# Two sets of feed-forward buffers, value products in pairs, and another order of loads and stages in a gated cross-attention kernel

## The chip, the cores and the metric

The program runs on one core of a Trainium2 chip. The time is the device time of one launch in microseconds (us), lower is better. Five engines work from queues of their own: TensorE (PE in the profile, its weight loads are PEld), VectorE (DVE), ScalarE (ACT), GpSimd (POOL) and SyncE (SP), which here only starts transfers and waits.

## The reference

Two gated blocks follow each other on x, which has 2 batches of 256 rows of 512 numbers. The context has 2 batches of 512 rows of 512.

```python
x = x + tanh(g_xattn[0]) * matmul(fake_quant(layernorm(x)), fake_quant(ctx))      # first sum
x = x + tanh(g_ffn[0])   * (W_base h + b + 0.5 * inverse_transform(adapters(h)))  # h = layernorm(x)
x = x + tanh(g_xattn[1]) * attention(layernorm(x), ctx, mask)   # 32 heads of 16, 8 key groups
x = x + tanh(g_ffn[1])   * bitlinear(relu(bitlinear(h, w_gate))**2 * bitlinear(h, w_up), w_down)
```

bitlinear rounds its input to 8 bits by the row's largest value, and its weights to -1, 0 and 1 by the mean of their absolute values. The weights are 1376 by 512, three of them.

## The kernel before, in words

The 512 rows are four tiles of 128. A stage is a tuple such as `("y0", 2, 1)`; one list of stages, `schedule()`, is walked by every engine, and each engine issues in that order the instructions that it has in a stage. So the list is the order of work on each engine, and semaphores join the engines. The list has `PREPARATION` first. Then come 128 steps of attention (4 heads of one key group of one tile are 4 steps): `s` makes the scores of one head on TensorE, VectorE reduces them to a maximum, `m` puts the maxima into the operand, `t` makes the scores again, transposed, and ScalarE takes the exponential, GpSimd clears masked places (`keep`) in the later half, and `pv` multiplies by the values. `FILL` says which other stages stand behind which step. Its keys go on above 152, where attention is over: there they only give an order, and I call that part the tail.

The stages that the change touches:

- `vt` multiplies the adapters' coefficients (after masks) by the transform's matrix, `we` multiplies that by the encoders, and VectorE adds the result to `wT`; `y0` uses it.
- `k` and `v` are keys and values; both need `wkvT` and the transposed context `ctx_T`. `ksplit` and `qsplit` split keys and queries into three bf16 parts, which go through DRAM. `qpick` brings the first heads' queries into place without DRAM.
- `cquant` quantises the context, `ln0`, `ln1`, `ln2`, `ln3` are the layer norms, `hT` a transpose.
- `fabs`, `fsum`, `fscale`, `fround`, `fclamp`, `fternary` make the three ternary weights out of `stage_w`, one after the other; `fload` 1 and 2 load the next matrix into the same `stage_w`.
- `f1T`, `gu`, `hidden`, `fq`, `f2T`, `y2`, `y2up` are the last feed-forward part of a tile: transpose the input, gate and up products in three pieces (512, 512 and 352 columns), gate times up and the row's maximum on VectorE, quantise, transpose, down product in three pieces, add to x and store.
- `y1` and `y1up` are the attention's output product and its addition to x.
- `warm` is a run of products of ones that nobody reads.

In the kernel before, a tile's gate values, quantised hidden values and both transposes have one buffer each (`gate`, `hid_q`, `hqT`, `hid_qT`), so a tile's stage waits for the tile before it to have left the buffer. The four down products cannot be put off, since the buffer must be emptied.

```python
if t:
    wait_filled(act, ("y2", t - 1))      # f2T: hid_qT of the tile before has been read
if t and stage[2] == 0:
    act.wait_ge(hid_q_ready, 2 * t)      # gu: gate of the tile before has been quantised
```

## Time and profile before

| what | value |
|---|---|
| median of 3 runs | 285.31 us (283.99 to 285.43) |
| the profiled execution | 285.12 us, span 283.3 us |
| mean granted TensorE clock | 0.976 of full speed |
| PE, DVE, ACT, POOL busy | 262.0, 211.9, 185.3, 115.4 us |
| bytes moved | 27.56 MB |
| first `s` matmul, last `pv` matmuls | 64.57 us, 244.35 us |

A time in a row is counted from the start of the span. The profile's lines name source lines: L622 is `vt`, L681 `q`, L706 `k`, L716 `v`, L671 `y0`, L738 `s`, L760 and L763 `t`, L787 `pv`, L810 `y1`, L828 `gu`, L836 `f2T`, L847 `y2`, L613 `warm` on PE. A float matmul stands as two instructions in the trace, so `vt`, which has four, is shown as x8. "Idle before" is the time for which the engine stood before an instruction, and what ended it.

### The profile page before, as it was taken

To read this page: it belongs to the slowest core of one execution; us is meant where nothing else is said; L and a number is where in the kernel's file an instruction comes from. 1 tells how busy PE (TensorE), PEld (TensorE's weight loads), DVE (VectorE), ACT (ScalarE), POOL (GpSimd) and SP (SyncE) were. 2 spreads that over 40 slices of the span, in tenths; PEclk is the share of its full clock that TensorE was granted. 3 is DMA by queue.
4 is the path that set the end of the run, shared out by engine and by line. 5 is a ranking of instruction groups with operands and counts; after the bars stand their busy time and mean duration, and the time that the engine had idled before them with its cause. 6 is when DMAs were issued, how large, how long until landed. Compare 5 with 4: busy or idle time off the path is not lost.

```text
span 283.3 us, 5004 instructions
## 1 busy us (share of the span) xinstructions
PE 262.0 (92%) x1617; PEld 128.4 (45%) x1640; DVE 211.9 (75%) x612; ACT 185.3 (65%) x311; POOL 115.4 (41%) x171
## 2 busy tenths in 40 slices
PE   8499899788899999999999999999999999899894
PEld 8326358545443343374244275324244253256581
DVE  3777956668887399886969962989988555969682
ACT  3602389568488989786589785888598577452232
POOL 3003304826311055575556475769646556100000
PEclk9879799999799999999999999999999999999999
DMA  6999945150592800057600000800001000000000
GB/s 182 410 409 417 373 191 111 38 102 21 132 364 81 141 0 2 1 194 281 102 0 3 0 2 3 156 9 1 5 0 39 0 0 3 0 37 2 37 2 37
DMA packets 7665, 27.56 MB, mean 97 GB/s; under 512 B 1344, under 2 KB 3952, under 8 KB 5880
## 3 DMA queue, kind: packets, MB, share of 16 engines
q1 hardware_dynamic: 7208, 21.55, 25.8%
q0 software_dynamic: 288, 5.70, 5.2%
q8 instruction: 13, 0.21, 0.3%
q14 instruction: 12, 0.10, 0.1%
q10 hardware_dynamic: 144, 0.00, 0.0%
HBM read 23.79 MB, written 3.41 MB: 96 GB/s over the span
## 4 chain that ended last, share of the span: by engine, by line
PE 73%; DVE 10%; ACT 10%; issue 5%; DMA 1%; POOL 0%; DVEq 0%; ACTq 0%
PE bank L760 10%; PE bank L787 10%; PE bank L738 10%; PE bank L671 5%; PE bank L681 5%; PE bank L828 5%; PE bank L763 4%; PE bank L810 4%; PE bank L847 3%; PE bank L746 3%; PE bank L706 2%; ACT big L968 2%; PE bank L613 2%; PE bank L622 2%; PE bank L716 2%
## 5 line engine op out<-in xcount | busy, mean ns | idle before, releaser
L1194 DVE CUSTOM_DVE_ANT_0 junk<-bank,maskb 128x512 bf16<-128x512 f32 x128 | 83.9, 687 | 19.7 <-PE bank L738 18.9
L968 ACT ACTIVATE big<-bank 128x512 f32<-128x512 f32 x128 | 74.5, 596 | 27.1 <-PE bank L760 11.6
L549 POOL TENSOR_TENSOR big<-big,product 128x512 int32<-128x512 int32 x48 | 61.6, 1284 | 49.6 <-ACT big L968 49.2
L738 PE MATMUL bank<-kst,qst 96*128 96x512 bf16 x128 | 48.9, 386 | 2.4 <-DVE mx L1194 1.6
L760 PE MATMUL bank<-qst,kst 99*128 99x512 bf16 x128 | 49.5, 386 | 0.9 <-ACT qst L951 0.5
L787 PE MATMUL bank<-big,vp 128*32 128x512 f32 x256 | 33.7, 604 | 1.5 <-POOL big L549 0.5
L738 PEld LDWEIGHTS bank<-kst,qst 96*128 96x128 bf16 x128 | 12.6, 99 | 33.9 <-issue 24.9
L763 PE MATMUL bank<-ident_b,maskb 128*128 128x512 bf16 x65 | 24.7, 380 | 0.0
L951 ACT ACTIVATE qst<-bank 3x512 bf16<-3x512 f32 x32 | 18.9, 590 | 7.0 <-PE bank L746 6.4
L760 PEld LDWEIGHTS bank<-qst,kst 99*128 99x128 bf16 x128 | 12.5, 98 | 21.8 <-ACT big L968 6.6
L828 PE MATMUL bank<-ternary,hqT 128*128 128x512 bf16 (+1 forms) x95 | 20.7, 356 | 1.2 <-ACT hqT L985 1.0
L559 POOL TENSOR_TENSOR mx<-mx 128x4 f32<-128x4 f32 x64 | 13.1, 204 | 20.8 <-DVE mx L1194 18.6
L671 PE MATMUL bank<-wT,hT 128*128 128x512 f32 x32 | 17.2, 644 | 2.5 <-ACT hT L908 1.7
L613 PE MATMUL bank<-ones_b 128*128 128x128 bf16 x280 | 18.3, 230 | 1.1 <-POOL ones_f L504 1.1
L613 PEld LDWEIGHTS bank<-ones_b 128*128 128x128 bf16 x280 | 17.7, 104 | 2.4 <-issue 1.1
L593 POOL TENSOR_SCALAR stage_w<-stage_w,wscale 128x1376 f32<-128x1376 f32 (+1 forms) x12 | 17.9, 1496 | 0.0
L681 PE MATMUL bank<-hT,wqT 128*128 128x128 f32 x128 | 17.3, 284 | 0.1
L681 PEld LDWEIGHTS bank<-hT,wqT 128*128 128x128 f32 x128 | 16.6, 198 | 1.1
L938 ACT ACTIVATE ternary<-stage_w 128x1376 bf16<-128x1376 f32 (+1 forms) x12 | 16.2, 1350 | 0.0
L810 PE MATMUL bank<-woT,aT 128*128 128x512 f32 x32 | 15.4, 592 | 0.0
L572 POOL TENSOR_TENSOR x<-x,product 128x512 f32<-128x512 f32 x3 | 3.9, 1307 | 25.4 <-ACT product L893 25.4
L828 PEld LDWEIGHTS bank<-ternary,hqT 128*128 128x128 bf16 x96 | 9.0, 97 | 10.9 <-ACT hqT L985 1.8
(167 smaller groups left out, 403.2 us busy)
## 6 DMA issues: line engine op xcount, KB each, us to landing
stage_w<-in_w_down POOLq DMA_DIRECT2D x1, 2816.0 KB, 11.5
stage_w<-in_w_gate SPq DMA_DIRECT2D x1, 2752.0 KB, 21.7
stage_w<-in_w_up POOLq DMA_DIRECT2D x1, 2752.0 KB, 12.1
...
```

The lines of the kernel that those rows point to most:

```text
L549: nc.gpsimd.tensor_tensor(p, p, keep[:, nt, KEEP_ST.index(i):KEEP_ST.index(i) + 1, :].broadcast_to([P, HG, P]), ALU.mult).then_inc(kept, 1)
L613: i = mm(o[:, 0:P], ones_b[:, :], ones_b[:, :], start=True, stop=True)
L671: i = mm(o[:, :], hT[:, k, :], wT[:, k, :], start=(k == 0), stop=(k == KT - 1))
L681: i = mm(o[:, c * P:(c + 1) * P], wqT[:, k, c * P:(c + 1) * P], hT[:, k, :], start=(k == 0), stop=(k == KT - 1))
L738: mm(o[:, :], qst[0:KS, tile % 2, g * HG + hh, :], kst[0:KS, tb(tile)[0], g, :], start=True, stop=True).then_inc(fill(stage), 1)
L760: i = mm(o[:, :], kst[0:KM, b, g, s * P:(s + 1) * P], qst[0:KM, tile % 2, g * HG:(g + 1) * HG, :], start=True, stop=by_keep(c, s))
L763: i = mm(o[:, :], maskb[:, nt, s * P:(s + 1) * P], ident_b[:, :, :], start=False, stop=True)
L787: i = mm(o[gi * VW:(gi + 1) * VW, :], vp[:, b * ST + s, (sc % 2) * 4 + gi, :], pt[:, gi, s, :], start=(s == 0), stop=(s == ST - 1))
L810: i = mm(o[:, :], aT[:, k, :], woT[:, k, :], start=(k == 0), stop=(k == KT - 1))
L828: i = mm(o[:, 0:n], hqT[:, k, :], tern[w][:, k * FF + c0:k * FF + c0 + n], start=(k == 0), stop=(k == KT - 1))
L968: fn(pt[:, c % 4, s, :], o[:, :], ACT.Exp).then_inc(drain(stage), 1)
L1194: v.tensor_tensor_reduce(junk[:, j % 2, :], o[:, :], maskb[:, tb(c // NG)[1], :], 1.0, HIDE, ALU.add, ALU.max, mx[:, c % 3, 0, hh:hh + 1]) ...
```

## The change

1. A second set of feed-forward buffers. Tiles 1 and 3 use parts of `stage_w` (free once all ternary weights are made) for `gate`, `hid_q` and `hid_qT`, and half of `hT` for `hqT`. Waits go to the tile two before. ScalarE waits before tile 1's first gate piece for all 12 ternary pieces. The output factor has a place for each tile, so that `y2up` can be late.
2. SyncE issues `wkvT` and the first transposed context (now in four pieces) ahead of the adapters' `coef`, `cmask` and `dft`; `enc` is loaded twice, behind a wait for a clearing by GpSimd.
3. `vt` runs in two halves of 64 columns, two blocks of the contraction side by side; `we` sums both by contracting over 128 partitions.
4. `pv` is issued in pairs, at steps 1 and 3 of each 16 instead of at 0, 1, 2 and 3.
5. `scalars` is split: context quantisation waits for the two reciprocals only.
6. `PREPARATION` and `FILL` are new orders. Banks that are taken before the attention and kept into it come from a set of their own. `fload` 2 moves from step 48 to 74. All seven `warm` runs stay, with the same counts (42, 60, 10, 10, 10, 74, 74), in other places.

```diff
-    1: [("q1T", 3)], 5: [("ksplit", 1), ("fternary", 0, 3), ("q", 1, 0)], 8: [("q", 1, 1), ("r", 3)],
...
+    0: [("ln2", 1, 5), ("fload", 1), ("v", 1, 3)], 1: [("vcopy", 1)], 2: [("hT", 1, 2)], 4: [("q1T", 3)],
...
-        if i >= 0 and i % 16 < 4 and i // 16 < NSC:
-            s.append(("pv", i // 16, i % 16))
+        if i >= 0 and i % 16 in (1, 3) and i // 16 < NSC:
+            s += [("pv", i // 16, i % 16 - 1), ("pv", i // 16, i % 16)]
...
+    late = list(range(S_BANKS, 8))
...
+        drained_at = at[drain_stage(use)]
+        if now < at[("s", 0)] < drained_at:
+            banks = late if drained_at < at[("t", 0, 0)] else late[T_BANKS:]
...
-        gate = hid[:, 0:FF]
+        gates = (hid[:, 0:FF], stage_w[:, 0:FF])
...
-        hid_q = hid[:, FF:FF + FT * P // 2].bitcast(BF16)
+        hid_qs = (hid[:, FF:FF + FT * P // 2].bitcast(BF16), stage_w[:, FF:FF + FT * P // 2].bitcast(BF16))
...
+            sp.dma_start(wkvT, wkvT_in).then_inc(ld_wkv, 16)
+            for k in range(KT):
+                sp.dma_start(ctx_T[:, 0, k], ctxT_in[0, :, k]).then_inc(ld_ctxT0[k], 16)
             sp.dma_start(coef, coef_in).then_inc(ld_coef, 16)
             sp.dma_start(cmask, cmask_in).then_inc(ld_coef, 16)
             sp.dma_start(dft, dft_in).then_inc(ld_dft, 16)
-            sp.dma_start(enc, enc_in).then_inc(ld_enc, 16)
+            sp.wait_ge(enc_cleared, 1)
+            for half in range(2):
+                sp.dma_start(enc[64 * half:64 * half + RR, :], enc_in).then_inc(ld_enc, 16)
...
-                    for k in range(KT):
-                        i = mm(o[0:RR, :], coef[:, k, 0, :], dft[:, k, :], start=(k == 0), stop=(k == KT - 1))
+                    for k in range(0, KT, 2):
+                        for half in range(2):
+                            i = mm(o[64 * half:64 * (half + 1), :], coef_rows[:, k + half, 0:64], dft[:, k + half, :], start=(k == 0),
+                                   stop=(k == KT - 2))
...
-                    act.wait_ge(scalars_ready, 1)
+                    act.wait_ge(scales_ready, 1)
...
-                    wait_filled(act, ("u", t - 1, 2) if t else ("p", NT - 1))
-                    fn(hqT[:, :, :], o.rearrange("p (k n) -> p k n", k=KT), ACT.Copy).then_inc(drain(stage), 1)
+                    wait_filled(act, (("p", NT - 1), ("q", NT - 1))[t] if t < 2 else ("u", t - 2, 2))
+                    fn(hqTs[t % 2][:, :, :], o.rearrange("p (k n) -> p k n", k=KT), ACT.Copy).then_inc(drain(stage), 1)
...
-                    if t and stage[2] == 0:
-                        act.wait_ge(hid_q_ready, 2 * t)
+                    gate = gates[t % 2]
+                    if t == 1 and stage[2] == 0:
+                        act.wait_ge(ternary_ready, 12)
+                    if t > 1 and stage[2] == 0:
+                        act.wait_ge(hid_q_ready, 2 * (t - 1))
```

The new list, where the prediction speaks of it. The end of the preparation is `y0` 1, `qpick` 0 and 1, `k` 1.3, `r` 2, `p` 2; `v` 1.3 and `hT` 1.2 now stand behind steps 0 and 2. The four `fabs` of the first weights stand in one row on ScalarE, ahead of `hT` 0.2. The order on TensorE after the last `pv` is: `gu` 1.2.0, `f1T` 2, `gu` 1.2.1, `oT` 7, `f2T` 0.0, `y1` 3.0, `aT` 3.1, `y1` 3.1, 3.2, `gu` 2.0.0, `y1` 3.3, `gu` 2.0.1, `f2T` 0.1, `gu` 2.1.0, `warm` of 74, `y2` 0.0, 0.1, `gu` 2.1.1, `f1T` 3, `gu` 2.2, `y2` 0.2, `gu` 3.0, `f2T` 1, `gu` 3.1, 3.2, `warm` of 74, `f2T` 2.0, `y2` 1, `f2T` 2.1, `y2` 2.0, 2.1, `f2T` 3.0, `y2` 2.2, `f2T` 3.1, 3.2, `y2` 3, `warm` of 10. In the kernel before, `f2T` 0, `y2` 0 and `gu` 1.2 are done within the attention, and the tail is `f2T` 1, `y2` 1, `f1T` 2, `oT` 7, `gu` 2, `y1` 3, `f2T` 2 with a `warm` of 74 in it, `y2` 2, `f1T` 3, `gu` 3, a `warm` of 74, `f2T` 3, `y2` 3.

## Rows read from the trace of the kernel before

**Rows 1.** The head of the page: span; each engine's busy us, share, instructions.

```profile
span 283.3 us, 5004 instructions
PE 262.0 (92%) x1617; PEld 128.4 (45%) x1640; DVE 211.9 (75%) x612; ACT 185.3 (65%) x311; POOL 115.4 (41%) x171
```

**Rows 2.** The chain that ended last, its shares of the span by engine.

```profile
PE 73%; DVE 10%; ACT 10%; issue 5%; DMA 1%; POOL 0%; DVEq 0%; ACTq 0%
```

**Rows 3.** Stretches: length, busy PE, PEld, DVE, ACT, POOL; granted clock, DMA share, GB/s.

```profile
11.60:64.50 52.90, 48.23 (x238) 27.20 (x240) 37.43 (x101) 26.49 (x43) 16.11 (x27) 0.90 0.69 240
64.50:244.30 179.80, 173.77 (x998) 73.22 (x1011) 140.88 (x415) 137.92 (x235) 97.00 (x131) 0.99 0.23 61
244.30:280.10 35.80, 32.44 (x287) 20.49 (x286) 26.61 (x75) 13.93 (x24) 0.00 (x0) 1.00 0.04 16
239.50:280.90 41.40, 37.24 (x321) 21.44 (x321) 31.82 (x84) 15.61 (x27) 1.55 (x2) 1.00 0.04 13
```

**Rows 4.** The timeline of TensorE up to the first steps of attention.

```profile
11.60 1.48 PE L636 MATMUL bank<-q,ones_b 128*128 128x512 bf16 x3 [2.91 <-ACT q L869]
...
16.13 4.72 PE L622 MATMUL bank<-hid,qst 128*40 128x512 f32 x8
...
40.01 1.11 PE L716 MATMUL bank<-mixed,big 128*128 128x128 f32 x8
...
54.99 1.10 PE L671 MATMUL bank<-wT,hT 128*128 128x512 f32 x2 [1.71 <-ACT hT L908]
...
63.52 0.66 PE L662 MATMUL bank<-ident_f,h 128*128 128x128 f32 x4 [0.89 <-DVE h L1050]
...
64.57 0.60 PE L738 MATMUL bank<-kst,qst 96*128 96x512 bf16 x2
...
71.46 0.39 PE L738 MATMUL bank<-kst,qst 96*128 96x512 bf16 x1 [1.22 <-DVE mx L1194]
```

**Rows 5.** SyncE's issue of the gate weights.

```profile
15.77 0.47 SPq L460 DMA_DIRECT2D stage_w<-in_w_gate  x1
```

**Rows 6.** The page's transfers: KB, median us from issue to landing.

```profile
stage_w<-in_w_gate SPq DMA_DIRECT2D x1, 2752.0 KB, 21.7
```

**Rows 7.** The timeline of ScalarE: first weights' sums, context, queries.

```profile
38.27 1.34 ACT L938 ACTIVATE ternary<-stage_w 128x1376 bf16<-128x1376 f32 x1
...
45.37 2.92 ACT L864 ACTIVATE big<-big,scr,cst 128x512 f32<-128x512 f32 x4
48.19 2.55 ACT L869 ACTIVATE q<-big,unround 128x512 bf16<-128x512 f32 x4
...
51.12 0.60 ACT L921 ACTIVATE qs<-bank 128x512 f32<-128x512 f32 x1 [0.38 <-PE bank L681]
```

**Rows 8.** The timeline of TensorE at the last value products.

```profile
240.10 1.07 PE L787 MATMUL bank<-big,vp 128*32 128x512 f32 x8
241.10 0.39 PE L760 MATMUL bank<-qst,kst 99*128 99x512 bf16 x1
...
241.64 2.78 PE L787 MATMUL bank<-big,vp 128*32 128x512 f32 x24
```

**Rows 9.** The timeline of TensorE in the tail.

```profile
244.35 0.62 PE L836 MATMUL bank<-ident_b,hid 128*128 128x128 bf16 x8
...
249.92 4.82 PE L828 MATMUL bank<-ternary,hqT 128*128 128x512 bf16 x24 [0.30 <-ACT hqT L985]
...
263.98 2.32 PE L847 MATMUL bank<-ternary,hid_qT 128*128 128x512 bf16 x10
...
271.92 4.29 PE L613 MATMUL bank<-ones_b 128*128 128x128 bf16 x74
```

**Rows 10.** The timeline of VectorE in the tail.

```profile
258.87 0.74 DVE L1209 SCALAR_TENSOR_TENSOR x<-bank,th,x 128x512 f32<-128x512 f32 x1
...
280.12 0.75 DVE L1293 SCALAR_TENSOR_TENSOR x<-bank,fs,x 128x512 f32<-128x512 f32 x1 [2.69 <-PE bank L847]
```

**Rows 11.** The columns of rows 3, for 4 us behind TensorE's wait of 2.91 us.

```profile
12.00:16.00 4.00, 3.31 (x15) 1.20 (x13) 3.01 (x7) 0.60 (x1) 0.00 (x0) 0.50 1.01 403
```

96 lines of the change are left out of this document (56 added, 40 removed), and 102 rows, old and new, of tables (FILL, PREPARATION).

## The prediction

> **What bounds the kernel now.** I read the head of the page first: TensorE is busy 262.0 of 283.3 us, VectorE 211.9 and the others less [rows 1]. The shares of the chain that ended last agree: 73% TensorE, 10% each for VectorE and ScalarE [rows 2]. A share over the whole is an average, so I cut the span by what goes on in it [rows 3]. The reader is to see three stages there. In the front (11.6 to 64.5) TensorE is busy 48.2 of 52.9 us, DMA is at 0.69. In the attention (64.5 to 244.3) it is busy 173.8 of 179.8, at a clock of 0.99, while VectorE has 140.9 and ScalarE 137.9. In the tail (244.3 to 280.1) it shows 32.4 of 35.8, but 148 of its products there are `warm`, 74 of them in 4.14 us (271.92 to the next work at about 276.05; the row says 4.29 with the drain) [rows 9], so about 8.3 us of that are cover for waits. Last I read timelines where stages meet. So the rule of this kernel is: in the attention, TensorE work that goes away is time; in the front and the tail, what counts is who is late.
>
> **The change, step by step.** The sum is made against the profiled execution: 285.12 us with a span of 283.3, 0.19 under the median of 285.31. The 1.8 us around the span and the end (the last `y2up` from 280.12, then the store to 283.3 [rows 10]) stay.
>
> *Loads and the front.* `wkvT` and the first transposed context, 1.5 MB, go ahead of the adapters' matrices, so `k` 0.0 and 0.1 can fill TensorE's 2.91 us of waiting at the context's sum [rows 4], and `vt` comes later. `vt` in two halves side by side: before, x8 take 4.65 us (16.13 to 20.78), the nearest rows for products side by side are those of `pv`, eight float instructions on four strips in 1.00 us [rows 4, 8]. Its bounds are 4.65 (nothing gained) and 2.33 (full overlap); I take 2.33. But neither this nor the earlier keys lie on the path, because of the gate weights. They are issued at 15.77 and land 21.7 later, at 37.5 [rows 5, 6], behind the same bytes in both orders. In the new list all four sums of them stand on ScalarE ahead of `hT` 0.2 and `qsplit`: 4 times 1.34 us [rows 7] plus the reading of the sum, say 5.3, so ScalarE is free at 43.0. Then a scaling (some 0.8), the copy for `hT` 0.2 (0.6, the size of the copy at 51.12 [rows 7]) at about 44.2 to 44.8, the second context's quantisation, 5.4 us (45.37 to 50.74 before [rows 7]), and `ln0r` 2 (0.7): the query split can begin at 50.9, against 51.12. So up to here 0.2 us are won, and TensorE only waits longer. The split's own length stays, so `y0` 1, which waits for the copy behind it, begins at about 54.6 instead of 54.99 [rows 4].
>
> From there to the first `s` it was 64.57 - 54.99 = 9.6 us. `v` 1.3 goes away from it (0.94, from the start of `v` 1.0 at 40.01 to the next product), `hT` 1.2 (0.5), its wait (0.89), the `warm` of 10 (0.56), `q1T` 2 (0.2); `k` 1.3 comes in (0.9). That is 7.4, and the first `s` is at 62.0: **-2.6**. `v` 1.3 and `hT` 1.2 move into the first steps, 1.4 us. There VectorE sets the pace (1.22 us wait at 71.46, behind the maxima [rows 4]), so between 0 and 1.4 is paid; I take **+0.7**. The new wait for GpSimd's clearing stands in SyncE's queue ahead of `enc`, `wT`, `bias`, x, `wqT`, the mask and the gate weights; the memset comes third on GpSimd, long before SyncE has issued the loads in front, so it costs nothing. If it were late, the gate weights would be. The same holds for the four issues that are added, since the transfers queue behind each other anyhow (DMA at 0.69 over the front, over 400 GB/s up to its middle [rows 11]).
>
> *Attention.* `f2T` 0, `y2` 0 and `gu` 1.2 leave it, `aT` 3.0 comes in. `y2` is 11 products of 0.22 us, 2.4 (the x10 take 2.32 [rows 9]); `f2T` 0.6; `gu` 1.2 twice 0.6, by 24 in 4.8 us [rows 9] and 352 columns of 512; minus 0.2 for `aT`. That is **-4.0** on the engine that is the bound.
>
> *Pairs.* One `pv` alone takes from 240.10 to 241.10, with 0.09 us of standing ahead of it: 1.09. Three in one row take 2.71 (241.64 to 244.35), 0.90 each [rows 8]. Each pair saves 0.19 us; the 32 stages make 16 pairs, and three already stood together: **-2.8**. TensorEngine Tiling, Key Properties, in the Trainium skill says that a change of tiling mode drains TensorE; the trace agrees in size and sign, the row gives the number.
>
> *What is given back.* Attention shrinks by 6.8 while the others' work stays: VectorE's 140.9 less about 3 (rows of `hidden`, `fq`, `y2up` that leave) over 173 us is 80%. It is not the bound on average, but in places. Nothing given back to 3.5 us is possible, I take **+1.0**. In it are two waits that ScalarE gets, each with all exponentials queued behind it: the sums of the down matrix 9 steps behind its load instead of 11, and all 12 ternary pieces at step 126.
>
> *Tail.* TensorE's busy time becomes 32.4 + 4.0 = 36.4 us. The second buffers let `y2` 0 and 1, `gu` 2 and 3 and `y1` 3 stand where it waited. Does a wait remain? After `y1up` 3 (258.87 [rows 10]) the norm to `f1T` 3's input takes about 7 us. In the new order TensorE has between `y1` 3.3 and `f1T` 3: two `gu` (1.7), `f2T` 0.1, `warm` (4.14), two thirds of `y2` 0 (1.7), one `gu` (0.9): 8.8. The last `warm` stands in front of 4.9 us of `y2` 1 and 2, while tile 3's quantising is under way. So both `warm` runs are partly in the way, and no wait is left: 36.4 against 35.8, **+0.6**. VectorE has 31.8 us in its stretch of 41.4 [rows 3] and gets about 5 more of it; it starts on tile 2's norm some 7 us before the last `pv`, so it is not late. A gain in the tail itself is possible only as far as busy time in the page holds drains, 1 us.
>
> Sum: -2.6 + 0.7 - 4.0 - 2.8 + 1.0 + 0.6 = -7.1, so 285.12 - 7.1 = **278.0 us**.
>
> **The rivals.**
> - *The others become the bound in attention* (they go round ScalarE's exponential, `keep` and `pv`): for it speaks that ScalarE and VectorE are at 77 and 78% there, against it that TensorE stood only 6.0 of 179.8 us. All 3.5 given back: 280.5 us. The case that the second buffers do nothing is close to it: the moved work then waits in the tail for VectorE, 281 us.
> - *The front gives nothing*, the first `s` stays at 64.5 because the split or its copies come later, or one slow stretch of TensorE's clock (below) takes 2.5 us of it back: 279.9 to 280.5 us.
> - *More is won*: `vt`'s 2.3 us or the keys reach the path (ScalarE is not held by the sums), and the attention gives nothing back: 274.5 us.
> - *Slower, by the clock.* TensorE will stand more in the front: after `we` for the first tile's norm (some 4 us) and before the sums' end (2 to 3 us). After the wait of 2.91 us the clock was 0.50 for 4 us, which is 1.2 GHz [rows 4, 11]; such a stretch of 5 us costs about 2.5 us if its work is on the path. Work of the queries and `y0` 1 is. To be slower by over 0.5% it must eat 8.5 us, so four such stretches more than now; all of the front from 43 us and the first steps at 1.2 GHz would give about 288 us. TensorE: Matmul & The Clock Gate, Part 1, in the Trainium skill says the same of its direction: the slow clock is the default state and comes back when the engine idles. By that rule at least one slow stretch is added here, which is the rival before this one, and rows 11 agree.
>
> **How the numbers follow.** Chances: forecast 0.38, others bound 0.18, front nothing or one slow stretch 0.20, more won 0.16, slower or nothing left by the clock 0.08. The range leaves out the last case and half of the best: bounds of the unknown terms are -2.8 and +4.5 us, which makes **274.3 to 282.5 us**. 0.5% is 1.4 us, about what a measurement of this kernel tells from no change. Only the clock's case reaches above 283.9: faster 0.89, same 0.05, slower 0.06.
>
> **What would show it.** Right: the first `s` at 61 to 63 us; the last `pv` at 235 to 238; TensorE busy 97% between; `pv` as x16 with starts 1.9 us apart; f2T, `y2` and `gu` without gaps in the tail, which is over 36 us long; ScalarE's sums from 37.6 in one row and TensorE standing before 43. Wrong: the first `s` at 64 or later (then look whether the query split or the clock was late), a clock of 0.5 to 0.7 in two or more stretches between 24 and 62, "ScalarE from the load of the down matrix" among the waits, an attention of over 176 us between first `s` and last `pv`, or gaps in the tail before `f1T` 3 or `f2T` 3.

## The result, and the profile of the changed kernel

| kernel | median, us | runs | lowest to highest |
|---|---|---|---|
| before | 284.65 | 4 | 282.66 to 285.43 |
| after | 271.75 | 4 | 270.89 to 272.65 |

The ratio is 0.9557 with a 95% interval of 0.949 to 0.9625: the kernel is 12.9 us faster by the medians. Forecast were 7.1 us and a range that ended at 274.3 us, so the sign was right and the size was not.

The head of the page and the chain that ended last, after, in the form of [rows 1, 2]:

```profile
span 270.8 us, 5030 instructions
PE 253.9 (94%) x1640; PEld 130.1 (48%) x1640; DVE 213.9 (79%) x613; ACT 185.3 (68%) x311; POOL 116.4 (43%) x172
...
PE 68%; ACT 4%; issue 2%; DVE 1%; ACTq 0%; DVEq 0%
```

VectorE, ScalarE and GpSimd are busy within 2 us as long as before; TensorE has 8.1 us less, and the chain goes less over VectorE (1%) and ScalarE (4%), where both had 10%. The three stages, with the columns of [rows 3], and behind them 8 us of the front:

```profile
11.60:64.00 52.40, 41.94 (x209) 25.03 (x209) 36.81 (x99) 27.03 (x43) 15.93 (x26) 0.93 0.71 245
64.00:232.10 168.10, 166.85 (x995) 73.21 (x993) 142.21 (x419) 135.87 (x233) 95.64 (x129) 1.00 0.24 63
232.10:267.30 35.20, 35.20 (x318) 23.07 (x315) 28.91 (x76) 15.69 (x27) 0.00 (x0) 1.00 0.06 23
44.00:48.00 4.00, 3.59 (x22) 3.59 (x23) 3.12 (x10) 3.54 (x8) 2.71 (x2) 0.70 1.00 193
48.00:52.00 4.00, 4.00 (x33) 4.00 (x33) 2.94 (x10) 3.80 (x7) 0.90 (x2) 0.88 0.03 4
```

I lay the execution out by three marks on TensorE: the first `s`, the end of the last `pv`, the end of the last `y2`. In the profiled executions they went from 64.57, 244.42 and 280.08 us to 64.03, 232.19 and 267.59. So the front gave 0.54 us, the attention 11.69 (179.85 became 168.16), the tail 0.26 (35.66 became 35.40). Nearly all of it came in the attention, where I had expected 5.1. TensorE's timeline after, with new line numbers (L636 is `vt`, L721 `k`, L740 the weights' sum `fscale`, L686 `y0`, L754 `s`, L776 and L779 `t`, L803 `pv`, L626 `warm`, L863 `y2`):

```profile
10.60 1.10 PE L721 MATMUL bank<-big,mixed 128*128 128x512 f32 x2 [1.39 <-DMA big<-in_ctxT]
...
17.89 3.35 PE L636 MATMUL bank<-hid,qst 128*64 128x512 f32 x8 [2.02 <-issue]
...
44.41 0.38 PE L740 MATMUL bank<-wtot,ones_f 128*128 128x1 f32 x2 [2.85 <-DVE wtot L1329]
...
57.08 3.67 PE L686 MATMUL bank<-wT,hT 128*128 128x512 f32 x8 [1.53 <-ACT hT L925]
...
64.03 0.38 PE L754 MATMUL bank<-kst,qst 96*128 96x512 bf16 x1
...
86.64 1.92 PE L803 MATMUL bank<-big,vp 128*32 128x512 f32 x16
...
228.51 3.68 PE L803 MATMUL bank<-big,vp 128*32 128x512 f32 x32
...
240.90 4.29 PE L626 MATMUL bank<-ones_b 128*128 128x128 bf16 x74
```

ScalarE in the front, in the form of [rows 7] (L955 the first sum, L938 the query split, L925 the copy that `y0` 1 waits for):

```profile
38.72 1.35 ACT L955 ACTIVATE ternary<-stage_w 128x1376 bf16<-128x1376 f32 x1 [1.71 <-DMA stage_w<-in_w_gate]
...
45.82 2.92 ACT L880 ACTIVATE big<-big,scr,cst 128x512 f32<-128x512 f32 x4
48.64 2.55 ACT L885 ACTIVATE q<-big,unround 128x512 bf16<-128x512 f32 x4
...
53.21 0.60 ACT L938 ACTIVATE qs<-bank 128x512 f32<-128x512 f32 x1 [1.40 <-PE bank L696]
...
56.36 0.58 ACT L925 ACTIVATE hT<-bank 128x512 f32<-128x512 f32 x1
```

### The profile page after: what moved, and what is told of

Its sections match the earlier page's. It is cut to its first block, busy times and chain, and to the rows that moved or that the text cites. A ratio compares the mean times of both kernels' runs of the same rounds, so it can differ in the third digit from the quotient of the medians.

```text
span 270.8 us, 5030 instructions
## 1 busy us (share of the span) xinstructions
PE 253.9 (94%) x1640; PEld 130.1 (48%) x1640; DVE 213.9 (79%) x613; ACT 185.3 (68%) x311; POOL 116.4 (43%) x172
## 4 chain that ended last, share of the span: by engine, by line
PE 68%; ACT 4%; issue 2%; DVE 1%; ACTq 0%; DVEq 0%
PE bank L776 11%; PE bank L803 10%; PE bank L754 9%; PE bank L844 7%; PE bank L779 6%; PE bank L826 5%; PE bank L696 4%; PE bank L863 4%; PE bank L762 3%; PE bank L626 3%; PE bank L686 2%; PE bank L811 1%; ACT ternary L955 1%; PE bank L852 1%; ACT big L985 1%
## 5 line engine op out<-in xcount | busy, mean ns | idle before, releaser
L776 PE MATMUL bank<-qst,kst 99*128 99x512 bf16 x128 | 48.9, 383 | 0.2
L754 PE MATMUL bank<-kst,qst 96*128 96x512 bf16 x128 | 48.0, 381 | 0.2 <-DVE mx L1215 0.2
L803 PE MATMUL bank<-big,vp 128*32 128x512 f32 x256 | 30.6, 598 | 0.0
L779 PE MATMUL bank<-ident_b,maskb 128*128 128x512 bf16 x80 | 30.4, 380 | 0.0
L754 PEld LDWEIGHTS bank<-kst,qst 96*128 96x128 bf16 x128 | 12.7, 99 | 22.4 <-issue 12.8
L572 POOL TENSOR_TENSOR mx<-mx 128x4 f32<-128x4 f32 x64 | 14.3, 223 | 20.5 <-DVE mx L1215 18.3
L776 PEld LDWEIGHTS bank<-qst,kst 99*128 99x128 bf16 x128 | 12.4, 97 | 20.6 <-ACT big L985 7.9
L606 POOL TENSOR_SCALAR stage_w<-stage_w,wscale 128x1376 f32<-128x1376 f32 (+1 forms) x12 | 17.2, 1439 | 6.9 <-DVE wscale L1337 6.9
L626 PE MATMUL bank<-ones_b 128*128 128x128 bf16 x280 | 18.1, 230 | 1.1 <-POOL ones_f L516 1.1
L626 PEld LDWEIGHTS bank<-ones_b 128*128 128x128 bf16 x280 | 17.6, 104 | 1.7 <-POOL ones_f L516 1.1
L955 ACT ACTIVATE ternary<-stage_w 128x1376 bf16<-128x1376 f32 (+1 forms) x12 | 16.2, 1349 | 1.7 <-DMA stage_w<-in_w_gate 1.7
L686 PE MATMUL bank<-wT,hT 128*128 128x512 f32 x32 | 15.4, 599 | 1.6 <-ACT hT L925 1.5
L803 PEld LDWEIGHTS bank<-big,vp 128*32 128x32 f32 x256 | 6.7, 109 | 16.7 <-issue 15.5
L963 ACT ACTIVATE ternary<-stage_w,unround 128x1376 bf16<-128x1376 f32 (+1 forms) x9 | 12.9, 1443 | 0.0
L762 PEld LDWEIGHTS bank<-ident_b,mx 128*3 128x3 bf16 x128 | 6.5, 86 | 13.3 <-issue 11.6
```

What stands on the lines that cost most here:

```text
L626: i = mm(o[:, 0:P], ones_b[:, :], ones_b[:, :], start=True, stop=True)
L686: i = mm(o[:, :], hT[:, k, :], wT[:, k, :], start=(k == 0), stop=(k == KT - 1))
L754: mm(o[:, :], qst[0:KS, tile % 2, g * HG + hh, :], kst[0:KS, tb(tile)[0], g, :], start=True, stop=True).then_inc(fill(stage), 1)
L776: i = mm(o[:, :], kst[0:KM, b, g, s * P:(s + 1) * P], qst[0:KM, tile % 2, g * HG:(g + 1) * HG, :], start=True, stop=by_keep(c, s))
L779: i = mm(o[:, :], maskb[:, nt, s * P:(s + 1) * P], ident_b[:, :, :], start=False, stop=True)
L803: i = mm(o[gi * VW:(gi + 1) * VW, :], vp[:, b * ST + s, (sc % 2) * 4 + gi, :], pt[:, gi, s, :], start=(s == 0), stop=(s == ST - 1))
```

## The experiments

The theory was that of the prediction, term by term; the rival theories were that the second buffers gave the large gain, that the pairs did, or that the new order removed waits which I had taken as given. Every kernel ran beside the kernel before, whose medians there were 284.01 to 285.13 us. The last three columns are the three marks above, from the one profiled execution of each kernel. Each product gets its PSUM bank (a piece of the memory that TensorE writes to) by its place in the list, so most edits of the list also deal these banks anew; only paired_first_steps against before_paired, one_set_rest_old, after_loads_old and vt_twice leave them as they were.

| kernel | median, us | ratio to before, 95% | first `s` | attention | tail |
|---|---|---|---|---|---|
| before_paired | 281.51 | 0.9908, 0.9875 to 0.9942 | 63.82 | 177.09 | 35.64 |
| paired_first_steps | 281.23 | 0.9862, 0.9814 to 0.9909 | 64.82 | 175.50 | 35.65 |
| front_new_rest_old | 278.08 | 0.98, 0.9771 to 0.9829 | 62.73 | 175.03 | 35.65 |
| one_set_rest_old | 278.08 | 0.977, 0.9728 to 0.9813 | 62.51 | 175.07 | 35.63 |
| y2_back_2 | 273.86 | 0.9616, 0.9558 to 0.9674 | 62.38 | 172.89 | 32.71 |
| y2_back | 277.77 | 0.9759, 0.9714 to 0.9804 | 62.40 | 170.63 | 39.22 |
| after_single_pv | 276.24 | 0.9735, 0.9709 to 0.9761 | 62.59 | 173.27 | 35.41 |
| v13_back | 271.59 | 0.9585, 0.9518 to 0.9653 | 63.77 | 167.25 | 35.40 |
| after_loads_old | 278.20 | 0.98, 0.9768 to 0.9833 | 68.58 | 168.10 | 35.41 |
| vt_twice | 270.96 | 0.9556, 0.9494 to 0.9618 | 62.12 | 168.18 | 35.41 |
| after_warm_gap | 273.76 | 0.9607, 0.9578 to 0.9637 | 63.28 | 169.34 | 35.40 |
| early_split | 276.42 | 0.9698, 0.9672 to 0.9724 | 64.16 | 170.99 | 35.40 |
| early_split_2 | 280.28 | 0.9874, 0.9819 to 0.9929 | 68.38 | 171.02 | 35.40 |
| early_split_2_no_warm | 276.14 | 0.9724, 0.9672 to 0.9776 | 67.78 | 171.01 | 32.06 |
| early_split_3 | 275.30 | 0.9672, 0.9632 to 0.9712 | 62.97 | 171.67 | 35.41 |
| early_split_3_no_warm | 272.59 | 0.9581, 0.9532 to 0.9629 | 64.13 | 170.00 | 32.01 |
| after_no_tail_warm | 267.99 | 0.9405, 0.9383 to 0.9428 | 62.53 | 168.10 | 31.96 |
| no_warm_f1T | 267.73 | 0.94, 0.9347 to 0.9454 | 62.86 | 168.09 | 31.96 |

### Pairs: before_paired and after_single_pv

The kernel before with pairs alone, and the kernel after without them:

```diff
-        if i >= 0 and i % 16 < 4 and i // 16 < NSC:
-            s.append(("pv", i // 16, i % 16))
+        if i >= 0 and i % 16 in (1, 3) and i // 16 < NSC:
+            s += [("pv", i // 16, i % 16 - 1), ("pv", i // 16, i % 16)]
```

> The kernel before, with its value products issued in pairs and nothing else. The prediction's step (0.19 us for each of 14 to 15 pairs that are new) expects 2.8 us less than the kernel before, a ratio of 0.990. The rival, that pairs also take away waits that stood around them, expects 5 us or more less, 0.983. That another engine is the bound in the attention expects no change.

> The changed kernel with the value products back at steps 0, 1, 2 and 3, one at a time. By the prediction's step: 2.8 to 3.0 us more than the changed kernel, 274.6 to 275. By the rival (pairs take away waits too): 276 or more.

In the old order the attention fell from 179.85 to 177.09 us: -2.76, where the sum had -2.8. In the new order the same edit is worth 5.1 us (173.27 against 168.16). The rest is waits that the first `pv` of a group has for GpSimd's clearing when it comes one step earlier; these rows of TensorE's timeline in `after_single_pv` are five of its eight groups:

```profile
129.51 1.07 PE L803 MATMUL bank<-big,vp 128*32 128x512 f32 x8 [0.17 <-POOL big L562]
...
149.23 1.06 PE L803 MATMUL bank<-big,vp 128*32 128x512 f32 x8 [0.34 <-POOL big L562]
...
173.82 1.07 PE L803 MATMUL bank<-big,vp 128*32 128x512 f32 x8 [0.22 <-POOL big L562]
...
192.95 1.06 PE L803 MATMUL bank<-big,vp 128*32 128x512 f32 x8 [0.28 <-POOL big L562]
...
211.42 1.07 PE L803 MATMUL bank<-big,vp 128*32 128x512 f32 x8 [0.82 <-POOL big L562]
```

They add up to 1.83 us, and all of TensorE's waits of over 0.15 us in the attention to 2.96 against 1.04 in after; 3.2 of the 5.1 us are left for the pairs and whatever else the edit moved. So an edit's worth depends on the order around it.

### The front and the first steps: front_new_rest_old

The kernel after, with its preparation and steps 0 to 25, and the list of the kernel before from step 26 on, tail included:

```diff
 FILL = {
     0: [("ln2", 1, 5), ("fload", 1), ("v", 1, 3)], 1: [("vcopy", 1)], 2: [("hT", 1, 2)], 4: [("q1T", 3)],
...
-    26: [("y0", 2, 0), ("fabs", 1, 0), ("y0", 2, 1), ("fabs", 1, 1), ("fabs", 1, 2), ("y0", 2, 2), ("fabs", 1, 3)],
+    26: [("fabs", 1, 0), ("fabs", 1, 1), ("fabs", 1, 2), ("y0", 2, 0)],
...
```

> The changed kernel's code (loads, vt in halves, pairs, second buffers in memory) with its PREPARATION and its FILL up to step 25, but the FILL of the kernel before from step 26 on. Both sets of stages are the same at that cut. If the surplus over the forecast came from the start of the attention (less standing, no slow clock there), this kernel has it: front 0.5, start 4, pairs 2.8, so about 277 to 278 us. If it came from the new order behind step 25 (gate, down product and norms moved), this kernel lacks it: 281 to 282 us. All the rest to 271.8 us is then the order and the tail that the second buffers allow.

Against before_paired the attention is 2.06 us shorter, though `v` 1.3 and `hT` 1.2 were pushed into it, for which the sum had +0.7. Where it came from is seen in the kernel before behind the wait of 1.22 us at 71.46 [rows 4]. This is its timeline there, and under the same fence its stretch from 72 to 76 us with the columns of [rows 3]:

```profile
69.10 1.05 PE L681 MATMUL bank<-hT,wqT 128*128 128x128 f32 x8
...
72.07 0.39 PE L738 MATMUL bank<-kst,qst 96*128 96x512 bf16 x1 [0.22 <-DVE mx L1194]
72.39 0.39 PE L746 MATMUL bank<-ident_b,mx 128*3 128x128 bf16 x4
72.71 1.86 PE L681 MATMUL bank<-hT,wqT 128*128 128x128 f32 x8
...
72.00:76.00 4.00, 3.71 (x16) 2.49 (x18) 2.82 (x11) 0.71 (x2) 2.33 (x4) 0.62 0.44 122
```

The query product takes 1.86 us where the one at 69.10 takes 1.05; the granted clock of these 4 us is 0.62 (it was 1.00 from 68 to 72). In front_new_rest_old the wait isn't there, `s` and `q` run on, and the same eight instructions and eight more take 2.05:

```profile
68.22 1.05 PE L698 MATMUL bank<-hT,wqT 128*128 128x128 f32 x8
69.11 0.64 PE L756 MATMUL bank<-kst,qst 96*128 96x512 bf16 x2
69.68 0.39 PE L764 MATMUL bank<-ident_b,mx 128*3 128x128 bf16 x4
70.00 2.05 PE L698 MATMUL bank<-hT,wqT 128*128 128x128 f32 x16
```

### Which places do it: paired_first_steps

In the list before, `ksplit` 1 stood behind step 5. On VectorE its two halves began at 68.71 and 70.10, among the maxima, and TensorE waited for the next maximum. These are the rows of the kernel before:

```profile
68.71 0.69 DVE L1167 TENSOR_TENSOR qs<-qs,parts 128x512 f32<-128x512 f32 x1
70.10 0.69 DVE L1169 TENSOR_TENSOR parts<-qs,parts 128x512 bf16<-128x512 f32 x1 [0.70 <-ACT parts L924]
```

The new list has it behind step 8, and `q` 1.3 behind 10 instead of 18. These two places alone, in before_paired:

```diff
-    5: [("ksplit", 1), ("fternary", 0, 3), ("q", 1, 0)], 8: [("q", 1, 1), ("r", 3)],
-    9: [("fload", 1)], 10: [("q", 1, 2)],
-    18: [("q", 1, 3), ("ln1", 2, 2), ("ln1", 2, 3)],
+    5: [("fternary", 0, 3), ("q", 1, 0)], 8: [("ksplit", 1), ("q", 1, 1), ("r", 3)],
+    9: [("fload", 1)], 10: [("q", 1, 2), ("q", 1, 3)],
+    18: [("ln1", 2, 2), ("ln1", 2, 3)],
```

> The kernel before_paired with two stages at the places that the new order has for them: the key split of batch 1 behind step 8 instead of 5 (on VectorE it stood for 2.0 us among the maxima, from 68.71 to 70.79, and TensorE then waited 1.22 us for a maximum), and the last query piece of tile 1 behind step 10 instead of 18. Theory: these two places are what took 2.1 us out of the attention in front_new_rest_old. The wait of 1.22 us and the slow clock behind it (0.62 from 72 to 76) go, the attention falls from 177.1 to 175.0 to 175.6 us, and the median from 281.5 to about 279.5. Rival: VectorE's work of the first steps is the bound wherever the split stands; the wait moves behind step 8, and the attention stays at 176.5 to 177.5.

The wait of 1.22 us is gone, the clock is 1.00 throughout, and the attention is 175.50 us: 1.59 of the 2.06. Three smaller waits came:

```profile
73.90 0.39 PE L760 MATMUL bank<-qst,kst 99*128 99x512 bf16 x1 [0.44 <-ACT qst L951]
...
77.50 0.39 PE L738 MATMUL bank<-kst,qst 96*128 96x512 bf16 x1 [0.56 <-DVE mx L1194]
...
84.35 0.39 PE L738 MATMUL bank<-kst,qst 96*128 96x512 bf16 x1 [0.39 <-DVE mx L1194]
```

They add up to 1.39 us, about what went (1.22 and another of 0.22). So the 1.59 us are not less waiting; they are the slow clock, which in before_paired was 0.58 from 72 to 76 us; an estimate from that is 0.42 times 4, 1.7 us.

The first `s` of this execution came 1.0 us later than that of before_paired, though nothing ahead of it was changed; its clock was 0.50 from 12 to 20 us, where before_paired had 0.74 and 0.83. The medians (281.23 and 281.51 us, ratios 0.9862 and 0.9908 with intervals that overlap) don't settle the 1.6 us by themselves.

### Is it the second set of buffers: one_set_rest_old, y2_back, y2_back_2

`one_set_rest_old` is front_new_rest_old with one set again:

```diff
-                    gate = gates[t % 2]
+                    gate = gates[0]
-                    if t > 1 and stage[2] == 0:
-                        act.wait_ge(hid_q_ready, 2 * (t - 1))
+                    if t and stage[2] == 0:
+                        act.wait_ge(hid_q_ready, 2 * t)
```

> The kernel of front_new_rest_old (new front, pairs, old order from step 26 on) with one set of feed-forward buffers again: every tile's gate, quantised hidden values and transposes in the first set, with the waits on the tile before. If the second buffers act only through the order that they allow: the same time, 278.1 us, within 0.7. If they take away waits in the old order too: 1 us or more slower.

The same median to the hundredth, and an attention within 0.04 us. The buffers do nothing in an order that doesn't use them. What their use is worth is told by putting the moved work back into the attention, in the new order:

```diff
-    164: [("gu", 1, 2, 0)], 213: [("gu", 1, 2, 1)], 235: [("f2T", 0, 0), ...], 495: [("f2T", 0, 1)],
-    581: [("y2", 0, 0)], 687: [("y2", 0, 1)], 811: [("y2", 0, 2)], 1526: [..., ("y2up", 0)],
+    130: [("f2T", 0, 0)], 132: [("f2T", 0, 1)], 135: [("y2", 0, 0)], 138: [("y2", 0, 1)],
+    140: [("y2", 0, 2), ("y2up", 0)], 144: [("gu", 1, 2, 0)], 148: [("gu", 1, 2, 1)],
```

> The kernel after, with its order from step 26 on, but with the work that left the attention put back into it: f2T 0 behind steps 130 and 132, y2 0 behind 135, 138 and 140 with its addition, gu 1.2 behind 144 and 148. So the tail loses 4 us of TensorE's work and the attention gains them; both warm runs of 74 stay where they are. Theory of the prediction (moved work is worth its size in the attention, and the tail has room only where it stood): attention 168.2 + 4.0 = 172.2, the tail 35.4 minus what isn't waited for instead. If all of the rest of the gain (2.9 of 6.9 us) is the order, attention is 172.0 to 172.5; if the other engines were the bound while that work stood in it, it is 173.5 to 175 (their waits come back with it). For the total: the tail of before stood 3.2 us. If the same waits come back in it, the time is after's plus 3 us, 274 to 275; if the new order of the tail needs them not, it is the same as after, 271 to 272.5, and moving the work was worth nothing by itself.

This ran into a wait of my own making. Tile 0's addition stood ahead of tile 2's normalisation on VectorE, and waited for `y2` 0.2 on a full TensorE; then `f1T` 2 made TensorE wait. VectorE first, then TensorE, of y2_back:

```profile
233.82 0.75 DVE L1319 SCALAR_TENSOR_TENSOR x<-bank,cst,x 128x512 f32<-128x512 f32 x1 [7.89 <-PE bank L863]
...
239.38 0.61 PE L833 MATMUL bank<-ident_b,hq 128*128 128x128 bf16 x4 [4.40 <-DVE hq L1261]
```

That is what the output factor of each tile's own is for: `y2up` can be late, and must be. In `y2_back_2` the addition stands behind the normalisation and the work further ahead:

```diff
-    132: [("f2T", 0, 1)], 135: [("y2", 0, 0)], 138: [("y2", 0, 1)],
-    140: [("y2", 0, 2), ("y2up", 0)], 144: [("gu", 1, 2, 0)], 148: [("gu", 1, 2, 1)],
+    131: [("f2T", 0, 1)], 133: [("y2", 0, 0)], 134: [("y2", 0, 1)], 137: [("y2", 0, 2)],
+    139: [("gu", 1, 2, 0)], 141: [("gu", 1, 2, 1)], 222: [("y2up", 0)],
```

> As y2_back, with two things mended: tile 0's addition stands on VectorE behind tile 2's normalisation (in y2_back it stood ahead of it, waited 7.89 us for y2 0.2, and f1T 2 then made TensorE wait 4.40 us), and all of f2T 0, y2 0 and gu 1.2 stands ahead of the last value products. If the late addition was the whole cause, attention is 168.2 + 4.0 = 172.2, f1T 2 waits little, and the tail is 35.4 - 4.0 + what y2 0 and gu 1.2 covered there. The norm of tile 3 reaches f1T 3 in after with nothing to spare beyond a warm run of 4.1 us, which is still there, so the tail should be 31.4 to 33.5 and the time equal to after's within 2 us: 271 to 274 us. If it is 275 or more, the work must be in the tail for the waits' sake.

Against the kernel after, the attention is 4.73 us longer and the tail 2.69 shorter: 2.04 more from the first `s` to the last `y2`. The medians say 2.1, but the intervals of the two ratios overlap (0.9558 to 0.9674 and 0.949 to 0.9625), so this size stands on the marks. By kind of stage, the attention's 4.73 are `y2` 2.46, `f2T` 0.61, one half of `gu` 1.2 0.71 (the other stayed behind the last `pv`) and 0.97 of waiting, which is one row: the second half of `f2T` 0, behind step 131, waits until ScalarE has copied the first.

```profile
221.68 0.33 PE L852 MATMUL bank<-ident_b,hid 128*128 128x128 bf16 x3 [0.99 <-ACT hid_qT L1024]
```

That wait comes from my choice of step, and a better one might lose it, which I did not run. So the buffers' use is worth about 2 us of the 12.9, and perhaps only 1. What is left between front_new_rest_old and y2_back_2, 2.14 us of attention and 2.94 of tail, is order alone (some 0.4 us of the first are the half of `gu` 1.2 that went to the tail). These are the stretches of attention and tail, first of front_new_rest_old:

```profile
62.73:237.76 175.03, 171.89 (x1025) 75.32 (x1024) 142.29 (x422) 137.64 (x236) 95.23 (x129) 1.00 0.23 62
237.76:273.40 35.64, 32.63 (x286) 20.46 (x286) 26.10 (x73) 13.81 (x24) 0.00 (x0) 1.00 0.04 16
```

and of y2_back_2:

```profile
62.40:235.30 172.90, 170.69 (x1022) 75.33 (x1021) 144.52 (x421) 138.17 (x237) 95.46 (x129) 1.00 0.23 62
235.30:268.00 32.70, 32.12 (x292) 20.85 (x293) 27.20 (x74) 13.16 (x23) 0.00 (x0) 1.00 0.07 25
```

Read busy against length: 3.1 and 3.0 us of standing became 2.2 and 0.6. Behind step 26, front_new_rest_old has five waits of over 0.15 us in the attention, all of them for ScalarE, 2.21 us together; y2_back_2 has two small ones (0.39) beside its 0.99. The reader also sees that VectorE's and ScalarE's busy time in the attention did not fall with its length, and nothing was given back for it.

### What was moved into the first steps: v13_back

```diff
-    ("k", 1, 3), ("fclamp", 0, 3), ...  ("ln2", 1, 4), ("p", 2),
+    ("k", 1, 3), ("v", 1, 3), ("fclamp", 0, 3), ...  ("ln2", 1, 4), ("p", 2), ("ln2", 1, 5), ("hT", 1, 2), ("vcopy", 1),
-    0: [("ln2", 1, 5), ("fload", 1), ("v", 1, 3)], 1: [("vcopy", 1)], 2: [("hT", 1, 2)],
+    0: [("fload", 1)],
```

> The kernel after, with the last value projection and the last transposition of tile 1 (v 1.3, hT 1.2), the last normalisation step of tile 1 and the copy of the values put back in front of the attention, where the kernel before has them: 1.4 us of TensorE's work leaves the first steps. My prediction's step: work pushed into the first steps costs 0 to 1.4 us there, so this kernel, which pays all of it ahead of the first s, would be 0 to 1.4 us slower, and the attention 0 to 1.4 shorter. What the runs since then say (the first steps of before stood behind VectorE's maxima and then had a slow clock, those of after don't): TensorE is the bound in the first steps of after too, so 1.4 us leave the attention (168.2 becomes 166.8), the first s comes 1.4 to 2 us later than 64.0 (hT 1.2 waits for VectorE's normalisation, up to 0.9 us), and the time is the same to 1 us slower: 271.5 to 273. The rival: the slow clock of the first steps comes back with the wait in front of hT 1.2, or the maxima become late again, and the attention doesn't get shorter: 273.5 to 275.

The attention is 0.91 us shorter, the first `s` about 1.2 later than in the seven profiled executions that have the preparation of after and a clock of 1.00 from 36 us to there (62.4 to 62.9 us), and the time is the same. The move is worth some 0.4 us. It explains nothing of the 2.06 us; rather, the work pushed in costs the attention 0.91 us, so that what else the new first steps took out is 3.0.

### The front: after_loads_old, vt_twice, after_warm_gap, the early splits

`after_loads_old` issues `wkvT` and the first transposed context where before had them, behind the adapters' matrices:

```diff
-            sp.dma_start(wkvT, wkvT_in).then_inc(ld_wkv, 16)
-            for k in range(KT):
-                sp.dma_start(ctx_T[:, 0, k], ctxT_in[0, :, k]).then_inc(ld_ctxT0[k], 16)
...
             sp.dma_start(bias[:, :], bias_in.partition_broadcast(P)).then_inc(ld_bias, 16)
+            for k in range(KT):
+                sp.dma_start(ctx_T[:, 0, k], ctxT_in[0, :, k]).then_inc(ld_ctxT0[k], 16)
+            sp.dma_start(wkvT, wkvT_in).then_inc(ld_wkv, 16)
```

> The changed kernel with the first transposed context and the keys' weights issued behind the bias again, as in the kernel before; the order of stages is kept, so k 0.0 stands ahead of the context's sum and waits for the load. If the loads' order is worth something in this order of stages: TensorE is held at k 0.0 until about 21 us instead of 10.6, and the norm of the first tile comes later by some 8 to 10 us; the gate weights' sums end at 44 us, so 3 us of that are hidden and 5 to 7 us show: 277 to 279 us. If the front is set by the gate weights alone: 272 us.

`k` 0.0 then holds TensorE's queue until its weights land:

```profile
19.89 2.07 PE L721 MATMUL bank<-big,mixed 128*128 128x512 f32 x2 [11.01 <-DMA mixed<-in_wkvT]
```

Of these 11 us, 4.6 (68.58 against 64.03) to 6.1 (against 62.5) reach the first `s`. The order of stages and the order of loads belong together; by itself neither tells its worth.

`vt_twice` issues the products of `vt` twice:

```diff
-                    for k in range(0, KT, 2):
+                    for k in (0, 2, 0, 2):
```

> The kernel after, with the four pairs of products of vt issued twice (the second set overwrites the first; the result is the same). It adds about 3.4 us of TensorE's work at 18 us. If vt lies off the path behind the sums of the gate weights, as the prediction has it, the first s stays within 0.5 us of 64.0 and the time within 0.5% of 271.8, only the 2.85 us of waiting at the weights' sum becomes less. If vt is on the path (the rival 'more is won': its 2.3 us reach the path), the first s comes 3 us later: about 275.

No later mark moved: the first `s` is at 62.12. `vt` is off the path, as the prediction had it. Its halves took 3.35 us in after, at a clock of 0.56 (17.89 to 21.24). At full clock they take 1.87 us up to the next product, as in y2_back_2, which is under my lower bound of 2.33; the 4.65 us from which I halved were themselves run at 0.76.

```profile
17.02 1.94 PE L636 MATMUL bank<-hid,qst 128*64 128x512 f32 x8 [1.46 <-issue]
```

`after_warm_gap` puts a `warm` of 50 into TensorE's wait of 2.85 us at 44.41:

```diff
-    ("fscale", 0),
+    ("warm", 0, 5, 50), ("fscale", 0),
```

> The changed kernel with a further run of 50 products of ones in front of the scale of the first weights (fscale 0), where TensorE stands 2.85 us and runs at a clock of 0.70 to 0.88 afterwards. If the slow clock behind that wait delays the queries and through them the first scores: 1 to 2 us less (first s at 62 to 62.7 instead of 64.0). If ScalarE's quantisation of the second context sets the query split anyway: no change.

The clock from 44 to 52 us was 1.00 instead of 0.70 and 0.88, but the first `s`, at 63.28, is no earlier than in the executions of after's preparation without that slow stretch, and TensorE then waited 1.59 us in the first steps for ScalarE's product of tile 2. The median is 2.0 us above that of after, though the intervals of the two ratios overlap:

```profile
66.14 0.60 PE L755 MATMUL bank<-kst,qst 96*128 96x512 bf16 x2 [1.59 <-ACT product L911]
```

That wait is a side effect of the edit. The `s` of step 1 needs the bank in which `p` 2 stands, and `p` 2 stands there because the added `warm` took a bank ahead of it: by the kernels' lists `p` 2 has bank 3 in after and bank 1 here, and the scores go through banks 0, 1 and 2.

The early splits put the query split of tile 0 ahead of the second context's quantisation on ScalarE (the core of the three diffs; `early_split_2` moves `ln0r` 2 behind `cquant` 1, `early_split_3` also `q1T` 2 and `ln0r` 2 behind `y0` 1 and `qpick`):

```diff
-    ("fsum", 0), ("ln0q", 2), ("fscale", 0), ("hT", 0, 2), ... ("cquant", 1), ... ("ln0r", 2), ... ("qsplit", 0),
+    ("hT", 0, 2), ("fabs", 0, 2), ("fabs", 0, 3), ("fsum", 0), ... ("qsplit", 0), ("ln0r", 2), ... ("cquant", 1),
```

> The changed kernel with another order in the front on ScalarE and TensorE: hT 0.2 stands behind the second of the four sums of the gate weights instead of behind the fourth, the first tile's query products and their split stand ahead of the second context's quantisation, and that context's column sum goes behind qpick. By the reading that the four sums and then the quantisation hold the query split: it starts some 5 us earlier and the first s at 59 to 61 us; with 1 to 2 us given back at the start of the attention the time is 3 to 4 us under the changed kernel, 268 to 269. If the keys' way through DRAM or tile 1's chain sets the first scores: 271 to 272.

> The kernel early_split, in which the query split of tile 0 begins some 6 us earlier because ScalarE's quantisation of the second context stands behind it, but with ln0r 2 (which waits for VectorE and held the copy of hT 1.1 there) put behind that quantisation. The copy of hT 1.1 is then at about 50.5 instead of 53.0, and y0 1 need not wait 3.4 us and run at half clock. Theory, the query split sets the first s: first s at 60 to 61, the attention 169 to 170 (p 2's product comes later and is waited for 1 to 2 us): 268 to 270 us. Rival, ScalarE's whole work up to the product for tile 2 (ln0r 2, quantisation, p 2) sets the start of the attention, wherever the split stands: the first s earlier, but its gain waited away in the first steps, 271 to 274 us.

> The kernel early_split_2 without the two runs of 74 products in the tail. As after_no_tail_warm against after, it should be 3.4 to 3.8 us less than early_split_2 if the tail is independent of the front: 264.5 to 266.5 by the theory, 267.5 to 270 by the rival. It is the candidate for the fastest of the study (after_no_tail_warm had 267.99).

> As early_split_2, but with the transposition of tile 2's first quantised rows (q1T 2) and ln0r 2 behind y0 1 and the picks of the queries, so that TensorE's y0 1 waits for the copy of hT 1.1 alone. It starts at about 51 instead of 57. Theory, the query split and what stands in TensorE's queue ahead of y0 1 set the first s: first s at 60 to 61.5 and the time 1 to 2.5 us under after: 269 to 271 us. Rival, ScalarE's sum of work up to tile 2's product and the first maxima sets it: the first s as early but the first steps wait 2 us more, 271.5 to 273.5 us.

> early_split_3 without the two runs of 74 products in the tail: 3.5 us under it, so 265.5 to 267.5 by the theory and 268 to 270 by the rival, against 267.99 of after_no_tail_warm.

Each moved the split 5 to 6 us ahead (47.1 to 48.0 us against 53.21 in after, and 51.59 in after_no_tail_warm, which lacks the slow stretch), and none won. In the first, ScalarE stood for VectorE in `ln0r` 2 with the copy for `y0` 1 behind it. In the second, `q1T` 2 stood in TensorE's queue ahead of `y0` 1 and waited 7.01 us for that same `ln0r` 2. In the third `y0` 1 was at 50.30 instead of 57.08, and the time was waited away behind it:

```profile
50.30 3.67 PE L687 MATMUL bank<-wT,hT 128*128 128x512 f32 x8 [0.60 <-ACT hT L926]
...
58.43 0.58 PE L659 MATMUL bank<-ident_b,hq 128*128 128x128 bf16 x4 [3.03 <-issue]
...
67.38 0.39 PE L755 MATMUL bank<-kst,qst 96*128 96x512 bf16 x1 [2.91 <-ACT product L911]
```

So an earlier split alone doesn't bring the start forward, and the theory that I tested with these kernels fell. What does set it they don't show, for two reasons. In all of them `p` 2 has bank 2, so that the `s` of step 2 waits for ScalarE's product (2.06, 2.05 and 2.91 us in the first, second and third), which in after, with `p` 2 in bank 3, it need not do. And each ran through two slow stretches where after had none: the first had a clock of 0.50 from 52 to 56 us and 0.62 from 68 to 72, the third 0.80 and 0.78 from 56 to 64 and 0.58 from 68 to 72. In the third ScalarE itself stood 2.20 us for VectorE ahead of that product, so its row of work isn't the whole cause either.

### The tail's warm runs: after_no_tail_warm, no_warm_f1T

```diff
-    522: [("gu", 2, 1, 0), ("ln3", 3, 3)], 535: [("warm", 3, 0, 74)], 541: [("ln3", 3, 4)],
+    522: [("gu", 2, 1, 0), ("ln3", 3, 3)], 541: [("ln3", 3, 4)],
...
-    976: [("warm", 3, 1, 74)], 981: [("f2T", 2, 0), ("y2", 1, 0)],
+    981: [("f2T", 2, 0), ("y2", 1, 0)],
```

> The changed kernel without the two runs of 74 products of ones in the tail, 8.3 us of TensorE. The prediction said that they are partly in the way and partly cover a wait. If the tail is set by TensorE alone: 8 us less. By the walk through the tail, VectorE's norm of tile 3 and its quantising then set it: some 3 us of wait at f1T 3 and 1 us at f2T 3, so 3 to 4.5 us less than the changed kernel, 267.5 to 269. If the clock falls in those waits, the gain is given back: 271 to 273.

267.99 us: it beats both kernels. The tail is 3.44 us shorter, though the runs took 8.3. TensorE waits for VectorE four times in it, and the clock stays at 1.00; three of the waits, and the whole tail with the columns of [rows 3]:

```profile
244.28 0.40 PE L833 MATMUL bank<-ident_b,hq 128*128 128x128 bf16 x4 [2.19 <-DVE hq L1261]
...
255.27 0.34 PE L852 MATMUL bank<-ident_b,hid 128*128 128x128 bf16 x3 [0.31 <-DVE hid L1311]
...
258.32 0.40 PE L852 MATMUL bank<-ident_b,stage_w 128*128 128x128 bf16 x4 [0.99 <-DVE stage_w L1311]
...
230.50:262.60 32.10, 28.14 (x171) 14.62 (x171) 28.78 (x76) 15.63 (x27) 0.00 (x0) 1.00 0.03 11
```

The clock is not safe, though. The two early splits without `warm` have the same tail and the same first wait (2.19 and 2.18 us), and behind it the clock fell in both. Here is early_split_2_no_warm, whose wait ended at 252.45; in early_split_3_no_warm the clock was 0.60 from 248 to 252 us:

```profile
252.00:256.00 4.00, 3.55 (x17) 1.83 (x18) 3.86 (x9) 1.56 (x3) 0.00 (x0) 0.70 0.00 0
```

Their tails are 32.06 and 32.01 us against 31.96, so the slow clock cost 0.1 us there: it only used up later waits for VectorE.

In `no_warm_f1T` half of `gu` 2.2 and `y2` 0.2 fill the first of these waits:

```diff
-    747: [("f1T", 3)], ... 809: [("gu", 2, 2, 0), ("gu", 2, 2, 1)],
-    811: [("y2", 0, 2)], 813: [("hidden", 2, 2)],
+    809: [("gu", 2, 2, 0)],
+    811: [("y2", 0, 2), ("f1T", 3)], 813: [("gu", 2, 2, 1), ("hidden", 2, 2)],
```

> The kernel after_no_tail_warm, in which f1T 3 made TensorE wait 2.19 us for VectorE's quantised rows, with the first half of gu 2.2 and y2 0.2 (0.6 and 0.65 us) put ahead of f1T 3, so that they fill the wait. The wait falls to about 0.9 us, the tail from 31.96 to 30.7, the time from 268.0 to 266.7. Rival: what comes behind f1T 3 (the copy of hqT for gu 3) isn't covered any more and the wait moves to gu 3, the same time within 0.3 us.

The wait fell from 2.19 to 0.95 us and came back behind it: the tail is 31.96 us in both. All of TensorE's waits in both tails are for VectorE, which is busy 28.8 of 32.1 us there, so a tail without `warm` seems to go by VectorE; no run with less work on VectorE tests that. The median of 267.73 us is the lowest of the study and not to be told from 267.99.

## Why the prediction was right or wrong, step by step

| step | forecast | measured | by |
|---|---|---|---|
| front, to the first `s` | -2.6 | -0.5; about -2 in executions without the slow stretch at 44 us | after; the seven others |
| first steps (work pushed in) | +0.7 | -2.1 (of it +0.9 for the work) | before_paired to front_new_rest_old; v13_back |
| pairs | -2.8 | -2.8 | before_paired |
| work that leaves the attention | -4.0 | -4.7 | y2_back_2 to after |
| given back by the other engines | +1.0 | -2.1 | front_new_rest_old to y2_back_2 |
| tail | +0.6 | -0.3 | before, after |

The measured column adds up to -12.5, which is the difference of the two profiled executions, 285.12 and 272.65 us. The forecast range had a slip of its own: -2.8 us from 278.0 is 275.2, not the 274.3 that I wrote. The wider bound missed too.

**The step that failed** is "what is given back", +1.0 us, and with it the +0.7 of the first steps. I wrote that attention shrinks while the others' work stays, and let their waits only grow. The waits and slow clock that the attention of before already had were part of the list's order, and the order was new. The first steps and the order from step 26 on took 2.1 us each out of it, where I had +0.7 and +1.0. That is 5.9 of the 6.6 us by which the attention was missed. In the first steps I named VectorE as the pace [rows 4] and priced only what comes in (rightly: +0.9 by v13_back), not that the query pieces stand in front of its wait, nor that the wait was made by a key split among the maxima, nor the clock behind it, which by paired_first_steps is 1.6 us of the gain. All could be read: 1.22 us of waiting, `ksplit` at 68.71 on VectorE, and 1.86 us for eight instructions that take 1.05. Behind step 26 what went are waits for ScalarE: 2.21 us of them in front_new_rest_old, and in after two waits of 0.4 us together.

**Work that leaves** was right in mechanism, at 3.8 us of moved work for one half of `gu` less than planned, with 1 us beside it, the wait for ScalarE's copy in y2_back_2.

**Pairs** were sized right. That they are worth 5.1 us in the new order, I had not seen. I wrote that the trace agrees in size with the rule of the drain; there was no size to agree with. The sentence of TensorEngine Tiling, Key Properties, in the Trainium skill, that a change of tiling mode drains TensorE, agrees in sign with both comparisons; it gives no number, the runs give 2.8 and 3.2 us for 16 pairs, and no run parts the drain from the rest.

**The front** was placed rightly, with its sums in one row and TensorE standing at 44, but they began at 38.72 and not at 37.6, and the first `s` was at 64.03 and not at 62.0. In y2_back_2, whose preparation is the same, TensorE stood 1.41 us there instead of 2.85 and the clock stayed at 1.00 (0.70 and 0.88 in after); its first `s` is at 62.38. It had its slow clock earlier, 0.50 from 28 to 32 us, where after has 1.00, so that TensorE reached the sum 1.2 us later and stood less. That is 1.65 us between two executions of one front, the rival "one slow stretch" with 1.65 of its 2.5 us. The runs of after fall into two pairs, 270.89 and 270.96, 272.55 and 272.65; the profile is of the slowest, and that the other pair lacked this stretch fits their distance but isn't shown.

**Tail.** Busy without a gap, as forecast, and 35.4 us long instead of over 36. That both `warm` runs are partly in the way was right: 3.44 of 8.3 us.

**Slower, by the clock** did not come: the mean granted clock rose from 0.976 to 0.987. TensorE: Matmul & The Clock Gate, Part 1, in the Trainium skill has the slow clock return when the engine idles; the waits of after show that (0.70 behind 2.85 us). A wait of 2.19 us was not followed by it in after_no_tail_warm and was in early_split_2_no_warm, in the same list of the tail.

**The buffers.** My sum gave their use -3.4 us (-4.0 and +0.6), the runs about -2.0, of which 1.0 is the wait at 221.68: the attention pays the work in full, and the tail takes back 2.7 of 4.7.

What stays open: which stages of the order from step 26 on removed the waits for ScalarE there. The move of `fload` 2 and of single stages was not tried alone, nor was an order with the PSUM banks held as they were. In the first steps 0.5 of the 2.06 us have no place found for them, or 1.4 us if the 0.9 of the pushed work is counted; in the traces that is waiting, 0.63 us before step 26 in front_new_rest_old against 1.91 in paired_first_steps.
